# A convolution and FFT network on one core: VectorE's order at the end of conv2

## What is computed

```python
for j in range(K.shape[0]):
    Kj = project(K[j])                      # K minus its mean over the 3x3 taps
    Lj = project(L[j])
    z = conv3x3(x, Kj)                      # conv1
    z = batchnorm(z, gamma[j], beta[j])
    z = jax.nn.relu(z)
    z = conv3x3T(z, Kj)                     # conv2
    x = x + h * z
    x = batchnorm(x, gamma[j], beta[j])
    x = diag_imp_conv_fft(x, Lj, h)         # fft2, times 1/(h|Lj^|^2+1), ifft2
```

## Time and profile before

| | us |
|---|---|
| median of 3 runs | 730.03 (729.81 to 731.03) |
| the profiled execution | 730.09 |
| its span, from the first to the last instruction | 728.0 |
| TensorE busy in it | 622.4 |
| VectorE busy | 505.8 |
| ScalarE busy | 344.0 |
| GpSimd busy | 233.1 |
| mean of TensorE's granted clock | 0.945 of full |

### The profile page before, as it was taken

One profiled execution on the slowest core, in us unless ns is written; L12 is line 12 of the kernel. 1 busy time (PEld: TensorE's weight loads), 2 busy tenths in 40 slices (PEclk: granted clock), 3 DMA queues, 4 the chain that ended last, 5 costly groups with the idle time before them and its releaser, 6 DMA issues.

```text
span 728.0 us, 14581 instructions
## 1 busy us (share of the span) xinstructions
PE 622.4 (85%) x5840; PEld 202.2 (28%) x5840; DVE 505.8 (69%) x875; ACT 344.0 (47%) x640; POOL 233.1 (32%) x180
## 2 busy tenths in 40 slices
PE   6498999999989669999896699998957989989863
PEld 3122333223322222233222222332212222323321
DVE  2679788965867866649678656497786563867664
ACT  1466666653973132339731323397313232982222
POOL 0367777760324602203145022032450220222200
PEclk9699999999999969999998799999987999999978
DMA  9993111119200050592000505910005059000044
GB/s 182 185 168 72 31 32 30 31 45 225 63 1 2 1 118 2 119 218 55 1 2 1 118 1 127 219 48 2 1 1 118 2 130 211 13 1 1 1 117 116
DMA packets 44786, 51.21 MB, mean 70 GB/s; under 512 B 36528, under 2 KB 36656, under 8 KB 42672
## 3 DMA queue, kind: packets, MB, share of 16 engines
q1 hardware_dynamic: 40240, 48.99, 31.5%
q10 hardware_dynamic: 4480, 1.30, 1.2%
HBM read 11.99 MB, written 4.19 MB: 22 GB/s over the span
## 4 chain that ended last, share of the span: by engine, by line
PE 55%; ACT 19%; DVE 16%; issue 6%; DMA 2%; SPq 1%; POOL 0%; DVEq 0%; ACTq 0%; POOLq 0%
PE psum L1019 29%; ACT Z L612 10%; PE psum L1091 6%; ACT work L634 5%; PE psum L1158 4%; DVE Z L947 3%; PE psum L1042 2%; PE psum L1187 2%; PE psum L1215 2%; PE psum L1230 2%; DVE work L920 2%; DMA X<-X 2%; PE psum L1212 2%; PE psum L1079 2%; DVE work L965 2%
## 5 line engine op out<-in xcount | busy, mean ns | idle before, releaser
L1019 PE MATMUL psum<-X,wts 128*32 128x512 f32 x1536 | 172.9, 598 | 6.9 <-DMA X<-X 4.9
L1019 PE MATMUL psum<-Z,wts 128*32 128x512 f32 x1536 | 172.4, 594 | 4.3 <-DVE Z L887 4.3
L473 POOL TENSOR_TENSOR Z<-X 128x512 f32<-128x512 f32 x64 | 80.8, 1287 | 252.9 <-DVE X L905 252.9
L634 ACT ACTIVATE work<-X,small 128x512 bf16<-128x512 f32 x128 | 90.7, 710 | 87.7 <-DVE X L905 87.7
L549 ACT ACTIVATE Z<-psum 128x512 f32<-128x512 f32 x64 | 38.2, 597 | 150.2 <-PE psum L1019 139.2
L483 POOL TENSOR_TENSOR X<-Z 128x1024 f32<-128x1024 f32 x24 | 56.7, 2386 | 138.5 <-DVE Z L947 138.5
L809 DVE BATCH_NORM_STATS2 stats<-Z 128x6 f32<-128x512 f32 x60 | 41.0, 691 | 70.6 <-ACT Z L549 70.5
L612 ACT ACTIVATE Z<-Z,small 128x512 f32<-128x512 f32 (+4 forms) x92 | 80.3, 922 | 5.2 <-DVE small L877 4.7
L1019 PEld LDWEIGHTS psum<-Z,wts 128*32 128x32 f32 x1536 | 50.2, 109 | 115.4 <-issue 106.9
L1019 PEld LDWEIGHTS psum<-X,wts 128*32 128x32 f32 x1536 | 47.8, 109 | 120.8 <-issue 110.1
L1158 PE MATMUL psum<-work,cstS 32*64 32x512 f32 x384 | 38.1, 751 | 47.5 <-DVE work L920 42.6
(11 more groups left out here) (127 smaller groups left out, 829.6 us busy)
## 6 DMA issues: line engine op xcount, KB each, us to landing
X<-X SPq DMA_DIRECT2D x64, 260.0 KB, 4.1
Z<-Z SPq DMA_DIRECT2D x32, 520.0 KB, 9.2
Z<-x SPq DMA_DIRECT2D x36, 128.0 KB, 4.2
out<-Z SPq DMA_DIRECT2D x24, 128.0 KB, 2.3
parS<-par SPq DMA_DIRECT2D x4, 673.0 KB, 11.6
Z<-x SPq DMA_DIRECT2D x12, 120.0 KB, 4.8
Z<-x ACTq DMA_DIRECT2D x14, 64.0 KB, 4.4
Z<-x SPq DMA_DIRECT2D x14, 64.0 KB, 5.0
```

The costliest lines, as they stand in the source:

```text
L473: nc.gpsimd.tensor_tensor(rows(Z0, REG, bp, CH * (2 * half + i), CH), low, high, op=op)\
L634: nc.scalar.activation(by_row(rest[:, o:o + N // 2].bitcast(bf16)), xc, what, bias=small[:, 26:27], accum_out=sums[:, NCH * i + c:NCH * i ...
L1019: last = nc.tensor.matmul(out_b[C * r:C * r + C, :], weights[:, o:o + C], rows(src, reg, bp, g, CH, dj - 1), start=(dj == 0), stop=(dj == ...
```

## The change

In the list of steps, "back" becomes a step of its own, and so do the weights. Behind conv2 the order was: moments, invW of pair 1 (with its transpose back), norm, affine of pair 0, turn of pair 3, affine of pair 1, fwdW of pair 3. It becomes: moments, norm, affine of pair 0, turn of pair 3, weights, invW of pair 1, back of pair 1, fwdW of pair 3; the affine of pair 1 goes behind conv1 step 0. The kernel sums (line 698) go behind conv2 step 13, and `prepare` holds the rest. GpSimd's unmix hangs on "back" now in place of "invW". The other pairs' "back" stands directly behind their "invW", as before.

```diff
-        12: fourier(j, 0, "invW"),
+        12: fourier(j, 0, "invW") + [("back", j, 0)],
...
-    steps += [("moments", j)] + fourier(j, 1, "invW") + [("norm", j, 2), ("affine", j, 0), ("turn", j, BP - 1), ("affine", j, 1)]
-    steps += fourier(j, 3, "fwdW") + fourier(j, 2, "invH")
+    steps += [("moments", j), ("norm", j, 2), ("affine", j, 0), ("turn", j, BP - 1), ("weights", j)]
+    steps += fourier(j, 1, "invW") + [("back", j, 1)] + fourier(j, 3, "fwdW") + fourier(j, 2, "invH")
     rest = {
+        0: [("affine", j, 1)],
         1: fourier(j, 3, "fwdH"),
-        2: fourier(j, 2, "invW"),
+        2: fourier(j, 2, "invW") + [("back", j, 2)],
         3: fourier(j, 3, "invH"),
-        5: fourier(j, 3, "invW") + [("affine", j, 2)],
+        5: fourier(j, 3, "invW") + [("back", j, 3), ("affine", j, 2)],
...
-                    elif what == "invW" and at[1] % Q == 0 and j + 1 < DEPTH:
-                        unmix_halves(j, at[1] // Q)
+                    elif what == "back" and j + 1 < DEPTH:
+                        unmix_halves(*at)
...
-            def prepare(j):
-                if j == 0:
-                    dve.wait_ge(consts_in, 16)
+            def sum_kernels(j):
                 dve.wait_ge(par_in, 16 * (j + 1))
                 link(nc.vector.tensor_reduce(ksum[:, :], parS[:, P_K:P_F].rearrange("p (k t o) -> p k o t", k=2, t=TAPS),
                                              op=ALU.add, axis=AX))
+
+            def prepare():
...
-                        elif j + 1 < DEPTH:
-                            dve.wait_ge(bn_ready, 2 * j + 2)
-                            prepare(j + 1)
-                            gamma_and_beta()
+                    elif what == "weights" and j + 1 < DEPTH:
+                        dve.wait_ge(bn_ready, 2 * j + 2)
+                        prepare()
+                        gamma_and_beta()
...
+                        elif at[1] == 13 and j + 1 < DEPTH:
+                            sum_kernels(j + 1)
...
-                    elif what == "invW" and at[1] % 2 == 0:
-                        move_back(j, at[1] // Q, at[1] % Q // 2)
+                    elif what == "back":
+                        for half in range(2):
+                            move_back(*at, half)
```

More of the change, by code:

```diff
@@ L168, in number_banks @@
     for step in steps:
-        if step in number or step[0] in ("turn", "affine", "moments"):
+        if step in number or step[0] in ("turn", "back", "affine", "moments", "weights"):
             continue
@@ L835, in _ @@
                 if c == 3:
-                    prepare(0)
+                    dve.wait_ge(consts_in, 16)
+                    sum_kernels(0)
+                    prepare()
                     gamma_and_beta()
```

## The result

| | before | after |
|---|---|---|
| median | 730.14 us (729.81 to 731.03, 4 runs) | 699.61 us (698.72 to 702.69, 4 runs) |
| ratio to before | 1 | 0.9587, 95% interval 0.9556 to 0.9619 |
| profiled execution | 730.09 us, span 728.0 | 700.20 us, span 698.4 |
| mean granted TensorE clock | 0.945 | 0.969 |

The changed kernel is faster by 30.5 us, where 27.2 us were forecast; when it was measured again beside the last experiments (e12) it was faster by 28.0 us. The two profiled executions differ by 29.6 us.

What follows compares the result with a forecast made beforehand. VectorE working alone at the end of conv2 while TensorE waits was taken as the bound; 25.35 or 23.13 us from three layers plus 4.0 or 1.8 from the last, middle 27.2, gave 702.9 us, eight in ten within 699.8 to 707.5.

Steps and rivals of the forecast that it cites:

- TensorE's order, banks and the hidden invW: End of conv2: norm matmul goes ahead of invW, which moves to banks 4 to 7; its delay costs nothing.
- the 3.3 us of cover: Layer 0: invW would end at 250.5, and VectorE would need its output only at 253.8.
- The norm, 3.78 us: VectorE, layers 0 to 2: norm falls from 5.58 to 1.80 us once unmix no longer runs beside it.
- Sums 1.18 us and weights 0.99 us: VectorE, layers 0 to 2: both leave the stretch before the turn, which starts earlier by these times.
- The bound of 1.1 us a layer: Main loop: cost if a reduction of the moved sums waited for GpSimd's unmix, 3.3 us in all; taken as zero.
- The turn 7.71 us earlier: VectorE, layer 0: turn starts at 250.40 instead of 258.11, so fwdW can start at 252.94.
- The two ends of the clock: Layers 0 to 2: gain per layer 8.45 us with TensorE's clock full at fwdW, 7.71 us with it down.
- the middle: Whole kernel: 27.2 us gain, between 24.9 us (clock down in all four layers) and 29.4 us (clock full).
- the 10 us of waits for the turn: TensorE before fwdW: its summed waits for VectorE's turn fall from 42.6 to about 10 us.
- The last layer, 1.8 or 4.0 us: Last layer, where only back 1 leaves the stretch: gain 1.8 us with the clock down, 4.0 with it full.
- given back: Rival, chance 0.08: something behind the transpose after fwdW doesn't move along, losing 2 to 3 us per layer; 709 to 712 us.
- the rival "slower": Rival, chance 0.02: second pair's rows reach X2 late for conv1 step 4, beyond about 6 us of slack.

Runs made afterwards that it cites:

- e12: The changed kernel itself measured again on the chip of the last experiments: 701.65 us, ratio 0.9619.
- e3: The kernel before, with GpSimd's unmix of pair 1 waiting until the weights are written, VectorE's order untouched: 718.34 us, ratio 0.9849.
- e3b: The kernel before, with GpSimd's unmix of pair 1 waiting for the norm's end, so over sums and weights: 725.61 us, ratio 0.9952.
- e1: Half the change to the kernel before: weights behind the turn, sums behind conv2 step 13, back 1 still ahead of the norm: 722.0 us, ratio 0.9911.
- e2: Other half of the change to the kernel before: norm first, back 1 last, sums and weights still between norm and turn: 711.39 us, ratio 0.9769.
- e8: The changed kernel with ScalarE's scaling of the second pair another two conv1 steps later: 699.93 us, ratio 0.961.
- e9: The changed kernel with two unread matmuls ahead of the norm's matmul and two ahead of the fourth pair's fwdW: 697.0 us, ratio 0.9557.
- e10: The changed kernel with conv1 step 0 ahead of the third pair's invH, in fwdW's first bank, plus two short fills of unread matmuls: 704.31 us, ratio 0.967.

## Why the prediction was right, and where not

- **TensorE's order, banks and the hidden invW.** Right. L866 starts 0.39 us behind L1139's start (0.42 forecast), and the delay of invW cost nothing, though invW itself took 3.60 us where I reckoned with 1.95: it ended at 252.28 in place of 250.5, and of the 3.3 us of cover 1.4 us were left.
- **The norm, 3.78 us.** Right in size (1.85 us against 1.80) and in cause; e3 and e3b show it without touching VectorE's order.
- **Sums 1.18 us and weights 0.99 us.** Right: e1 gives 1.98 to 2.42 us a layer for both. The sums at their new place cost nothing, with 0.87 us left where I had written 0.8. The bound of 1.1 us a layer for a reduction that waits for GpSimd didn't come; e3b shows a reduction beside unmix at its usual length.
- **The turn 7.71 us earlier.** It came to 250.34 against 250.40.
- **The two ends of the clock.** Both are real: the upper in the changed kernel (8.33 to 8.52 us against 8.45), the lower in e2 and in layer 0 of e8 (0.82 us less against 0.74). The step that was mis-sized in layers 0 to 2 is the choice of the middle between them. I took the three layers at 25.35 or 23.13 us and expected some of each; they came to 25.35 us in the profiled execution. I had argued from the two gaps as if the clock would fall before fwdW or not at all. It fell sooner, behind the first gap, and so was back in time. In that case neither transform is paid for, because invW is covered. Eight of nine such stretches of the changed order show it (the changed kernel, e8, e12), so the middle was too low. The same slip stands behind the 10 us of waits for the turn, which were 4.0.
- **The last layer, 1.8 or 4.0 us.** 2.43 us: the lower end's case (fwdW 3.72 us), and some of the follow-up at a better clock (L1218 took 3.75 us against 4.65). e9 has the full clock there and 1.6 us more, which makes 4.0.
- **What was not in the sum.** 1.8 us of the 29.6 come from a fall of the clock behind a transfer of X, in the execution of before that was profiled. The prediction looked for the clock only at the end of conv2. The fall is no part of the change: it comes and goes in both orders. Where the measured gain passes the forecast by this, that is chance, and the change measured twice gave 30.5 and 28.0 us.
- **The rivals.** Nothing was given back: the stretches behind conv1 have their old length. The slack of the second pair was taken too small (6 us, and 8.1 are there), so the rival "slower" was farther away than I wrote.

The sum, with what was measured: 25.35 + 2.43 + 1.82 = 29.6 us, against 27.2. About 1.1 us of the 2.4 us is the clock in layers 0 to 2, 1.8 us the fall in before's conv1, and the last layer was 0.5 us under the middle of its two ends.

**What stays open:** whether the packet of code is what makes the transfer of X longer without fills (5.46 us against 3.89 in layer 2), and what decides in an execution at which point of a gap or behind it the clock falls. Neither was separated by a run. Nor was it tried to put the turn ahead of the norm, though the turn waits for nothing that the norm writes.

## What to carry to other kernels

When one engine works alone at the end of a stage, list its steps and ask of each who waits for it: here only the turn fed TensorE's next transform, and three of the other four could move behind it or away. Before you believe a step's length, find the same instruction elsewhere in the trace; if it is ten times shorter there, look for what runs beside it and move that away, as moving back 1 did here to unmix. Work left in the order behind such a stage should first go where its own cover is, as invW and the transform under L933 show: moved out of its cover (e10), a hidden 1.95 us became a paid one.

## What the runs showed of the hardware

- The granted clock fell behind a gap of 2.58 us in which TensorE did nothing and behind which only a matmul of 5 columns stood before invW. It did so in all four layers of the changed kernel, but not at the same point: over most of invW in layers 0 to 2 (3.60, 3.61 and 3.41 us), only in its middle in the last (2.47). Two matmuls of 0.93 us in each gap were enough to keep it full in all four layers (e9). Behind a wait of 2.4 to 3.0 us for a transfer it fell in four of ten executions.
- The lower clock cost something only where the transform is not covered: invW at 3.60 us in place of 1.95 changed nothing, fwdW at 3.7 in place of 1.98 costs 0.8 us in layers 0 to 2.
- GpSimd's unmix (two instructions of 2.35 us) stretched a 128x1 VectorE instruction from 0.16 to 2.08 us and the four 128x96 ones of the weights from 1.01 to 4.18 us, but not the reduction (1.18 us), and not the transposes out of PSUM (2.47 us beside unmix).
- A transfer of X of 260 KB took 5.2 to 5.8 us in the ten executions in which a packet of the instruction queue fell into it, and 3.9 us in the four in which none did, at the same place of layer 2.
